# Output stage of a two-branch cross attention: class-token rows of tiles 2 and 3 as a second matmul addend, and a reload split in three

## The reference

```python
query = x @ Wq;  keyt = enc @ Wk;  valt = enc @ Wv        # enc: the first 124 context tokens
hs = mha(query, keyt, valt)                               # 2048 x 640, scores 2048 x 124 a head
ca_q1 = einsum('btc,th->bch', ca, Wq_ca)[:, indices, :]   # 384 rows, spread over 2048
ca_hs1 = mha(ca_q1, x, x)
ca_hs2 = mha(ca_hs1 @ Wq, ca @ Wk_ca, ca @ Wv_ca)         # 4 keys a head
out = (hs + ca_hs2) @ Wout + b_out + x
```

## Time and profile before

| What | Value |
|---|---|
| Runs of the kernel | 767.13, 768.8, 770.88 us (median 768.8) |
| The profiled execution | 769.75 us, span 768.0 us, granted TensorE clock 0.982 |
| Busy: PE, PEld | 725.4 us (94%), 677.1 (88%) |
| Busy: DVE, ACT, POOL | 564.1 us (73%), 375.9 (49%), 171.4 (22%) |
| Output stage of batch 0, of batch 1 | 282 to 417 us, 642 to 768 us |
| DMA | 227021 packets, 82.37 MB; 208324 packets under 512 B |

### The profile page before, as it was taken

How to read it: one execution, slowest core, us unless ns; L and a number is a source line. 1 busy time by engine, 2 the same in 40 slices (tenths; PEclk the granted TensorE clock), 3 DMA queues, 4 the chain that set the end, 5 groups by cost and what they waited for, 6 DMA issues and landing times.

```text
span 768.0 us, 12603 instructions
## 1 busy us (share of the span) xinstructions
PE 725.4 (94%) x4693; PEld 677.1 (88%) x4693; DVE 564.1 (73%) x952; ACT 375.9 (49%) x942; POOL 171.4 (22%) x205
## 2 busy tenths in 40 slices
PE   7998999999899996968999999999999999799998
PEld 5978999999788886968899999999978887699997
DVE  3456888888899997436674888888889998656562
ACT  1634544454588962222333544455479994142330
POOL 8024951222100003502210521111110002211220
PEclk9999999999999999888999999999999999899999
DMA  8424353333400046697754334444230005578852
GB/s 275 144 94 124 69 125 90 90 90 90 145 30 1 0 76 157 137 218 183 151 139 101 65 90 109 102 98 94 90 129 2 0 1 128 131 159 188 177 124 74
DMA packets 227021, 82.37 MB, mean 107 GB/s; under 512 B 208324, under 2 KB 210372, under 8 KB 226960
## 3 DMA queue, kind: packets, MB, share of 16 engines
q1 hardware_dynamic: 226960, 81.56, 43.4%
HBM read 50.06 MB, written 31.39 MB: 106 GB/s over the span
## 4 chain that ended last, share of the span: by engine, by line
PE 80%; DVE 8%; SPq 3%; DMA 3%; issue 3%; ACT 2%; POOL 0%; DVEq 0%; POOLq 0%
PE PS L1230 30%; PE PS L1435 13%; PE PS L1418 6%; PE PS L1205 6%; PE PS L1305 6%; PE PS L1336 6%; PE PS L1327 5%; PE PS L1177 2%; SPq L432 2%; PE PS L1142 2%; DMA exT<-p_kept 2%; DVE pT_lo L1047 1%; SPq L479 1%; DVE res L1063 1%; PE PS L1188 1%
## 5 line engine op out<-in xcount | busy, mean ns | idle before, releaser
L1230 PE MATMUL PS<-mm_hi,xT_hi 128*128 128x280 f32 (+3 forms) x480 | 159.5, 332 | 0.0
L890 DVE TENSOR_REDUCE mpart<-PS 128x4 f32<-128x512 f32 x192 | 131.6, 687 | 36.9 <-PE PS L1205 36.7
L1230 PE MATMUL PS<-mm_hi,xT_lo 128*128 128x280 f32 (+3 forms) x480 | 157.4, 328 | 0.0
L1230 PE MATMUL PS<-mm_lo,xT_hi 128*128 128x280 f32 (+3 forms) x480 | 156.5, 326 | 0.0
L560 POOL TENSOR_TENSOR ex<-ex,rinv 128x992 f32<-128x992 f32 x30 | 55.4, 1845 | 201.5 <-DVE rinv L884 201.4
L666 ACT ACTIVATE ex<-PS,neg 128x124 f32<-128x124 f32 x256 | 89.9, 364 | 11.7 <-DVE gs L872 6.4
L1230 PEld LDWEIGHTS PS<-mm_hi,xT_hi 128*128 128x128 f32 x480 | 90.2, 188 | 0.7 <-issue 0.5
L1230 PEld LDWEIGHTS PS<-mm_lo,xT_hi 128*128 128x128 f32 x480 | 90.4, 188 | 0.3
L1230 PEld LDWEIGHTS PS<-mm_hi,xT_lo 128*128 128x128 f32 x480 | 90.3, 188 | 0.3
L754 ACT ACTIVATE oT_hi<-PS 128x256 fp32r<-128x256 f32 x80 | 29.5, 384 | 121.7 <-PE PS L1418 121.1
L608 POOL TENSOR_TENSOR xin<-xin,bias 128x640 f32<-128x640 f32 x32 | 49.8, 1562 | 160.6 <-DMA xin<-in_x 160.6
(11 more groups left out here) (154 smaller groups left out, 1355.9 us busy)
## 6 DMA issues: line engine op xcount, KB each, us to landing
ex_kept<-ex SPq DMA_DIRECT2D x32, 512.0 KB, 2.9
ex<-ex_kept SPq DMA_DIRECT2D x112, 128.0 KB, 3.1
xin<-in_x SPq DMA_DIRECT2D x128, 80.0 KB, 2.9
xin<-in_x SPq DMA_DIRECT2D x32, 320.0 KB, 3.5
out<-res SPq DMA_DIRECT2D x32, 320.0 KB, 2.3
raw_kept<-raw SPq DMA_DIRECT2D x5, 512.0 KB, 2.6
ex<-ex_kept SPq DMA_DIRECT2D x4, 512.0 KB, 3.8
mm_lo<-raw_kept SPq DMA_DIRECT2D x10, 186.0 KB, 4.4
```

What stands on the lines that cost most here:

```text
L890: nc.vector.tensor_reduce(mpart[:, n // 2, :, 2 * (n % 2):2 * (n % 2) + 2, i].rearrange("p s k -> p k s"), PS[:, 6 + N % 2, :].rearrange(" ...
L1230: last = mul(PS[:, slot(T, k), p0:p0 + w], l[:, i % 2, j, :], rr[:, m0:m0 + w], start=(j == 0 and n == 0), stop=(n == 2), skip_group_check ...
```

## The change

- Tiles 2 and 3 get their image rows as tiles 0 and 1 do. The selection matmul has 512 columns for four tiles; ScalarE copies them to `p2T` and a new `p2T2`; `heads_T(1)` uses 124 rows and adds a matmul of `vcab` and `p2T2` to each of its five parts. Their `gather`, `take_p2c`, `keep_image` and image read are gone: three chunks are left. GpSimd's columns for the next batch wait until `vcab` is read.
- TensorE: nT(1) and nT(2) stand inside output(0, 0), before its fourth part, for after it; the gather of tiles 4 to 7 stands behind output(0, 1) and waits for p2s, for inside group 1.
- VectorE, group 0: after soft2(1) come blocks_T(4), probs2(1), add_x(0), blocks_T(5); add_x(1) stands in group 1 between the second and third oT_lo.
- ScalarE: take_p2c(0) behind soft2(1) in group 0, take_p2c(1) and (2) behind oT_hi of groups 1 and 2.
- SyncE: the block loads of tiles 4 and 5 come before the write back of the last tile, each waiting for a transpose; keep_image(0) and image_rows(2) between the stores of group 0; the block loads of tiles 2g+6 and 2g+7 come behind the stores and the image read of group g.
- The reload of the score matrix: 6, 6 and 3 DMAs behind the block loads of groups 1, 2 and 3, with a semaphore each. next_high and next_low: four in groups 3 to 5 and three in group 6, for three in groups 2 to 6.

The diff, cut to its core:

```diff
--- before.py
+++ after.py
@@ -44,7 +44,8 @@
-CHUNKS = ((2, 4), (4, 8), (8, 12), (12, 16))
+STACKED = 4
+CHUNKS = ((4, 8), (8, 12), (12, 16))
...
@@ -185,6 +186,9 @@
+        with (nc.sbuf_tensor("ns1_room", [P, 2, CAD], F32), nc.sbuf_tensor("p2T_room", [3 * NH * NT, G2], F32R),
+              nc.sbuf_tensor("e0_room", [P, EW], F32), nc.sbuf_tensor("p2T2", [3 * NH * NT, G2], F32R) as p2T2):
+            pass
...
@@ -455,28 +460,32 @@
-                keep_image(0)
+                for i in range(STACKED, STACKED + 2):
+                    sp.wait_ge(exT_made, b * (TILES - OWN) + i - STACKED + 1)
+                    load_blocks(i)
                 sp.wait_ge(norm_made, (b + 1) * TILES)
                 sp.dma_start(ex_kept[b, TILES - 1], last_ex()).then_inc(last_out, 16)
-                image_rows(1)
                 for g in range(GROUPS):
-                    if g + 2 < GROUPS:
-                        if 2 * g + 6 == TILES:
-                            sp.wait_ge(last_out, (b + 1) * 16)
-                        load_blocks(2 * g + 4)
-                        load_blocks(2 * g + 5)
                     store(2 * g)
+                    if g == 0:
+                        keep_image(0)
+                        image_rows(2)
                     store(2 * g + 1)
-                    if g + 1 < GROUPS - 1:
-                        if g < len(CHUNKS) - 1:
-                            keep_image(g + 1)
+                    if 1 <= g < GROUPS - 2:
+                        if g < len(CHUNKS):
+                            keep_image(g)
                         image_rows(g + 2)
-                    if g == 1 and b + 1 < B:
+                    if 2 * g + 6 == TILES - 2:
+                        sp.wait_ge(last_out, (b + 1) * 16)
+                    if g < GROUPS - 3:
+                        for i in range(2 * g + 6, 2 * g + 8):
+                            load_blocks(i)
+                    if 1 <= g < 4 and b + 1 < B:
                         sp.wait_ge(raw_out, KT * 16)
                         sp.wait_ge(nT_ps, CT * (b + 1))
-                        for j in range(KT):
+                        for j in ((0, 1), (2, 3), (4,))[g - 1]:
                             for k, (h0, h1) in enumerate(((6, 8), (0, 3), (3, 6))):
-                                sp.dma_start(mm_heads(mm_lo, j, k).bitcast(F32), raw_kept[:, j * NH + h0:j * NH + h1, 0:NK]).then_inc(raw_in, 16)
+                                sp.dma_start(mm_heads(mm_lo, j, k).bitcast(F32), raw_kept[:, j * NH + h0:j * NH + h1, 0:NK]).then_inc(raw_in[g - 1], 16)
...
@@ -615,6 +624,7 @@
                     if b == 0 and i == 3:
+                        pool.wait_ge(oT_ps, 2 * KT)
                         g_columns(1)
                         y_columns(1)
...
@@ -728,16 +738,20 @@
                     else:
-                        act.wait_ge(image_in, (b * (GROUPS - 1) + i // 2) * 16)
+                        if i < STACKED:
+                            act.wait_ge(exT_made, b * (TILES - OWN) + i - OWN + 1)
+                        else:
+                            act.wait_ge(image_in, (b * (GROUPS - 2) + i // 2 - 1) * 16)
...
 
                 def take_p2T():
-                    act.wait_ge(p2c_ps, b * len(CHUNKS) + 1)
-                    nc.scalar.activation(p2T[:, :], PS[0:3 * NH * NT, 5, 0:G2], ACT.Copy).then_inc(p2T_made, 1)
+                    act.wait_ge(p2T_ps, b + 1)
+                    for to, at in ((p2T, 0), (p2T2, G2)):
+                        nc.scalar.activation(to[:, :], PS[0:3 * NH * NT, 5, at:at + G2], ACT.Copy).then_inc(p2T_made, 1)
 
                 def take_p2c(n):
-                    (i0, i1), (bank, at) = CHUNKS[n], ((5, G2), (4, 0), (5, 0), (4, 0))[n]
+                    (i0, i1), (bank, at) = CHUNKS[n], ((4, 0), (5, 0), (4, 0))[n]
...
@@ -752,8 +766,6 @@
                         nc.scalar.activation(oT_hi[:, j, :], PS[:, oT_bank(g, j), 0:G2], ACT.Copy).then_inc(oTh_made, 1)
-                        if g == 1 and j == 2:
-                            take_p2c(1)
 
...
@@ -766,22 +778,21 @@
                 soft2(0)
                 take_p2T()
-                take_p2c(0)
                 for g in range(GROUPS):
                     oT(g)
                     if g == 1:
+                        take_p2c(1)
+                    if g == 2:
                         take_p2c(2)
-                    if g == 2:
-                        take_p2c(3)
                     if g + 1 < GROUPS:
                         pT(2 * g + 2)
                         pT(2 * g + 3)
                     if g == 0:
                         soft2(1)
+                        take_p2c(0)
                     if b + 1 < B:
-                        if g == 2:
-                            act.wait_ge(raw_in, 3 * KT * 16)
-                        for n in range(3 * g - 6, 3 * g - 3) if 2 <= g < 7 else ():
+                        for n in range(4 * g - 12, min(4 * g - 8, 3 * KT)) if 3 <= g < 7 else ():
+                            act.wait_ge(raw_in[n // 6], (6, 6, 3)[n // 6] * 16)
                             next_high(n)
...
         @block.vector
@@ -1049,6 +1060,8 @@
 
                 def oT(g):
                     for j in range(KT):
+                        if g == 1 and j == 2:
+                            add_x(1)
...
@@ -1091,12 +1104,15 @@
                         soft2(1)
-                    add_x(2 * g_)
-                    if g_ == 0:
+                        dve.wait_ge(pTl_made, b * TILES + STACKED)
+                        blocks_T(4)
                         probs2(1)
-                        add_x(1)
+                        add_x(0)
+                        blocks_T(5)
+                    else:
+                        add_x(2 * g_)
                     if b + 1 < B:
-                        for n in range(3 * g_ - 6, 3 * g_ - 3) if 2 <= g_ < 7 else ():
+                        for n in range(4 * g_ - 12, min(4 * g_ - 8, 3 * KT)) if 3 <= g_ < 7 else ():
                             next_low(n)
...
@@ -1105,7 +1121,7 @@
-                    if g_ + 2 < GROUPS:
+                    if 1 <= g_ < GROUPS - 2:
                         dve.wait_ge(pTl_made, b * TILES + 2 * g_ + 4)
...
@@ -1347,16 +1363,18 @@
-                    (i0, i1), (bank, first) = CHUNKS[n], ((5, G2), (4, 0), (5, 0), (4, 0))[n]
-                    if n >= 2:
-                        pe.wait_ge(p2c_made, b * len(CHUNKS) + n - 1)
+                    (i0, i1), (bank, first) = CHUNKS[n], ((4, 0), (5, 0), (4, 0))[n]
+                    if n == 1:
+                        pe.wait_ge(p2T_made, 2 * (b + 1))
+                    if n == 2:
+                        pe.wait_ge(p2c_made, b * len(CHUNKS) + 1)
...
                             last = mul(PS[0:NH * NT, bank, at:at + w], p2s[:, c, lo, :], sel[:, ms[0]:ms[-1] + 1, :].rearrange("p m n -> p (m n)"),
-                                       skip_group_check=True, start=(n > 0 and c == blocks[0] and lo == 0), stop=(c == blocks[-1] and lo == 1))
+                                       skip_group_check=True, start=(c == blocks[0] and lo == 0), stop=(c == blocks[-1] and lo == 1))
                     last.then_inc(p2c_ps, 1)
...
@@ -1398,11 +1416,10 @@
                     pe.wait_ge(p2l_made, 2 * b + 1)
-                    mul(PS[0:3 * NH * NT, 5, 0:G2], p2s[:, 0].rearrange("p m n -> p (m n)"), sel[:, 0:OWN, :].rearrange("p i n -> p (i n)"),
-                        start=True, stop=True, skip_group_check=True)
-                    gather(0)
+                    mul(PS[0:3 * NH * NT, 5, :], p2s[:, 0].rearrange("p m n -> p (m n)"), sel[:, 0:STACKED, :].rearrange("p i n -> p (i n)"),
+                        start=True, stop=True, skip_group_check=True).then_inc(p2T_ps, 1)
...
-                    pe.wait_ge(p2T_made, b + 1)
+                    pe.wait_ge(p2T_made, 2 * b + 1)
                     for j in range(KT):
...
@@ -1413,14 +1430,15 @@
                         pe.wait_ge(oTl_made, (b * GROUPS + g) * KT + j - 1)
...
                             pe.wait_ge(tmp_made, CT * b + 2 + j)
+                        rows = NK if g == 1 else P
                         for n, (vv, pp) in enumerate(((vs_hi, pT_hi), (vs_lo, pT_hi), (vs_hi, pT_lo))):
                             for k, (h, c0, c1) in enumerate(pieces[j]):
-                                last = mul(PS[:, 6 + j % 2, 0:G2], strip(vv, j, h), pp[:, h, :],
-                                           start=(n == 0 and k == 0), stop=(n == 2 and k + 1 == len(pieces[j])))
+                                last = mul(PS[:, 6 + j % 2, 0:G2], strip(vv, j, h)[0:rows], pp[0:rows, h, :],
+                                           start=(n == 0 and k == 0), stop=(g > 1 and n == 2 and k + 1 == len(pieces[j])))
+                        if g == 1:
+                            pe.wait_ge(p2T_made, 2 * (b + 1))
+                            last = mul(PS[:, 6 + j % 2, 0:G2], vcab[:, j * P:(j + 1) * P], p2T2[:, :], start=False, stop=True)
                         last.then_inc(oT_ps, 1)
```

(20 more changed lines are left out.)

## The result

The changed kernel takes 757.23 us (median of 4, 756.51 to 758.37) against 769.4 of the kernel before beside it (median of 4, 767.13 to 770.88): ratio 0.9846, 95% interval 0.9823 to 0.9869. It is faster, by 1.5%, but by 12 us and not 22, and lies outside my range of 741.5 to 753. The profiled execution took 756.88, with a span of 755.2 and a mean clock of 0.993.

What follows compares the result with a forecast made beforehand. Bound: busy TensorE; only its waits (21.2 us for VectorE's oT_lo) and slow clock give time. 15.0 - 0.3 + 10.2 + 0.4 - 1.2 - 1.7 - 0.1 = 22.3 us gained: 746.5 against median 768.8, range 741.5 to 753.

Steps and rivals of the forecast that it cites:

- group 0 to 1, batch 0: First output matmul of tile pair 0 to that of pair 1: 16.3 us instead of 23.96, gaining 7.7.
- group 2, both batches: Third tile pair: late block loads cost 0.15 us per batch (-0.3); batch 1's old 0.5 wait goes (+0.4).
- group 3: Fourth tile pair, batch 0: block loads ahead of any reload part remove the stall, 14.98 us for 4.75 of work: +10.2.
- group 4: Fifth tile pair, batch 0: late SyncE and VectorE's work make TensorE wait 0.2 to 1.8 us, taken as -1.2.
- group 5: Sixth tile pair, batch 0: TensorE's wait grows to 3.2 us from 1.69, costing 1.7.
- pT_lo starts at 291.9 and ends 2.36 later: VectorE, tiles 2 and 3, batch 0: without the image read, pT_lo ends at 294.2 instead of 298.9.
- TensorE gets to the gather at 290.35 + 8.80 + 0.6: Batch 0: after 60 output matmuls and eight nT, TensorE reaches the gather at 299.8, then waits 0.5 us for p2s.
- land near 314.5, just in time: 0 to 0.5 us of wait in group 2: Block loads of tiles 6 and 7, behind store(1): 0 to 0.5 us wait, taken as 0.15 per batch.
- 4.0 + 15.6: Image read issued 4.0 us after output, then 15.6 to VectorE's oT_lo; less 15.2 cover and 1.2 already waited: 3.2 wait.
- the new wait costs the clock too: Rival, chance 0.25: the 3.2 us wait in group 5 also lowers the clock, losing 2 to 6 us: 749 to 753.
- The prediction's estimate of 750: Two image reads, taken to land after 4 us, could each come up to 1.8 us later, giving 750.
- Not faster: Rival, chance 0.03: each of three reload parts stalls TensorE by 10.2 us, 30.6 against 25.6 gained: 774.

Runs made afterwards that it cites:

- experiment 1: Changed kernel with GpSimd's first three bias additions of each batch held until VectorE's pT_lo of tiles 2 and 3: 760.01 us, ratio 0.9863.
- experiment 2: Kernel before, GpSimd's first bias addition waiting for pT_hi of tile 2, so the additions run beside VectorE's pT_lo: 772.3 us, one run.
- experiment 8: Changed kernel with fixes combined: bias additions after pT_lo, early loads of tiles 6 and 7, reload in five parts of three, first_keys in group 6: 744.28 us.
- experiment 7: Changed kernel with each of its three reload parts ahead of its group's block loads instead of behind: 759.83 us, one run.
- Experiment 5: Changed kernel with bias additions after pT_lo, tile 6's loads ahead of image_rows(2) and tile 7's right behind store(1): 754.45 us, ratio 0.9787.
- experiment 4: Changed kernel without the 15 reload DMAs, GpSimd writing zeros in their place: 752.63 us, one run.
- experiment 9: Changed kernel with only the reload recut, five parts of three DMAs behind groups 0 to 4, three subtractions in groups 2 to 6: 753.22 us, ratio 0.9784.
- experiment 6: Changed kernel with all 15 reload DMAs in one block behind group 1's block loads: 763.29 us, one run.
- experiment 3: Changed kernel with VectorE's first_keys for the next batch moved from group 4 to group 6: 756.67 us, ratio 0.9822.
- 11: Combined kernel (all fixes together) with GpSimd's wait for pT_lo removed again: 746.79 us, ratio 0.9692.

## Why the prediction was wrong

The direction and the places were right; three sizes were not. Against the forecast's sum, from the two timelines (us gained):

| term | forecast | measured |
|---|---|---|
| group 0 to 1, batch 0 | +7.7 | 23.96 - 18.36 = +5.6 |
| group 0 to 1, batch 1 | +7.3 | 23.58 - 18.59 = +5.0 |
| group 2, both batches | -0.3 + 0.4 | -0.5 - 1.0 = -1.5 |
| group 3 | +10.2 | +10.2 |
| group 4 | -1.2 | -1.4 |
| group 5 | -1.7 | 6.3 - 11.4 = -5.1 |
| group 6, and slow start of output(5) | -0.1 | -0.2 |
| sum | 22.3 | 12.6 |

The two spans differ by 12.8.

**Step "pT_lo starts at 291.9 and ends 2.36 later": failed.** The start was right and the duration was not. I took it from a row in which GpSimd was idle and moved the instruction into 4.59 us of add_bias; I had counted GpSimd's new wait and not its old work. Experiments 1 and 2 show it from both sides. The next steps held: from pT_lo's end to the last p2s 6.06 us (295.87 to 301.93) for 6.0, and from gather to output 6.4 for 1.2 + 4.75 + 0.35 = 6.3. In batch 1 most of it stands in the wait: 2.41 for the 0.5 forecast, and 18.6 for 16.3. Alone the two take 2.36 + 4.59 = 6.95 us, together 6.58 from the first start to the last end, so they hardly overlap. The Trainium skill, "SBUF — State Buffer", Who interferes with whom, says that a VectorE instruction with two SBUF inputs contends with a GpSimd instruction that reads SBUF, and calls the port pair that they share an exclusive lock; the trace agrees. The prediction did not reckon with it.

**Same sum, "TensorE gets to the gather at 290.35 + 8.80 + 0.6": failed in batch 0.** It took 11.3 us without the wait, for 9.7 in batch 1, because the clock stood at 0.50 for 3.4 us. That is why p2s was waited for only 0.66 there: a slow TensorE hid a late VectorE. The kernel before has 1.00 in that stretch of both batches. What drops the clock there is open. It fell in no batch of the kernel before and of experiment 2, and in 12 of the 22 batches of the changed kernel and the runs made from it: both in experiments 1 and 8, none in 7, one of the two in every other. In the changed kernel's batch 0 the waits ahead of output(0) hardly differ from before: 0.47, 0.56 and 0.76 us for 0.46, 0.56 and 0.64.

**Step "land near 314.5, just in time: 0 to 0.5 us of wait in group 2": under-sized.** 0.54 and 1.52. The loads stood behind image_rows(2), whose read waits for the write of p_kept: 2.96 us, not 1.6. Experiment 5 removes it.

**Step "4.0 + 15.6" of group 5: its mechanism right, its size wrong.** Issue at +4.4 instead of 4.0, landing 5.68 instead of 4, VectorE's 11.6 as forecast: 21.7, less the 15.2 of cover and the 1.5 already waited in group 4, makes 5.0; it waited 4.83 instead of 3.2. Then the clock, 0.50 over 6.8 us, which is the rival "the new wait costs the clock too" (0.25): true, but with 756.9 beyond its 749 to 753, since the other steps failed too. The prediction's estimate of 750, for reads up to 1.8 later, took its size from the latency at high load in the Trainium skill, "DMA: Bandwidth & Descriptors", Latency and other measured facts; the read of group 5 landed 1.7 later than the 4 that I took, so in size that estimate was nearer for this term. That memory latency is the cause no run shows. Experiments 4 and 9 show that the reload part ahead of the read is: without it, or with three DMAs in it, 4.1 and 4.0.

**Right:** group 3 to a tenth; group 4 (1.50 us of wait for 1.2, of which experiment 4 puts 1.2 down to the reload part); "Not faster" refuted; no loss in the later groups of batch 1. **Wrong in the weighing:** each step had a cover of under 1 us, and I gave the errors as independent of one another in a range 11.5 us wide, where late DMA moves groups 2, 4 and 5 together.

## What to carry to other kernels

An instruction that is moved brings its duration only if the other engines' work at the new place is the same: look up what GpSimd does there before a VectorE operation with two SBUF inputs is moved, and the other way round. The same holds for the fix: GpSimd's additions, held back behind pT_lo, met the next such VectorE operation, a small one (0.23 us became up to 1.50), where the chain could not spare it. A transfer taken off the head of a queue should be cut so fine that a part ends before the next short, urgent read is due; here 15 reload DMAs in parts of three cost the combined kernel no wait in groups 3 to 5, in parts of six about 5 us there (1.2 and 3.8, experiment 4), and as one block 9 to 10, ahead of the loads (14.98 for 4.75) or behind them (336.7 to 359.6 from output to output in experiment 6, for 13.5). A wait that a fix removes may reappear as a low clock or as the next wait, so judge a fix together with the others: GpSimd's wait alone brought nothing (760.0 for 757.2), in the combined kernel 2.5 us by the medians, with overlapping intervals.

## What the runs showed of the hardware

- VectorE's pT_lo (two of 128x1024, both inputs in SBUF) takes 2.36 us alone, 4.21 to 4.77 beside add_bias that began first, 3.73 where the two began within 0.2 us; add_bias (three of 128x640) 4.59 alone and 6.4 to 6.6. A subtraction of 128x64 with both inputs in SBUF takes 0.23 alone and, where add_bias runs already, ends with it: 0.57 to 1.50. Two multiplications of 128x192 with one input in PSUM take 0.80 to 0.85 either way.
- In the chains of these runs an image read lands after 3.3 to 4.6 us with no reload or a part of three ahead, and after 4.75 to 6.27 with six just ahead of it and the stores.
- How long a wait must be to cost the clock had no sharp edge. It stayed whole behind waits of 1.50, 2.05 (experiment 3), 2.26, 2.38, 2.41, 2.57 and 2.87 us, and fell behind 1.80 (experiment 9), 2.14 (11), 2.75 (1), 2.94, 3.28, 3.52, 4.06 and 4.83. 2.05 us also cost it in experiment 7, whose window from 2 us behind that wait shows 0.56, the 1.2 GHz level; the second line is the window behind the 1.80 of experiment 9:

```profile
355.90:359.30 3.40, 3.40 (x17) 3.40 (x17) 0.85 (x2) 1.40 (x3) 0.76 (x1) 0.56 1.00 236
...
665.50:668.90 3.40, 3.40 (x20) 3.40 (x21) 0.95 (x3) 0.77 (x2) 1.41 (x1) 0.66 0.77 229
```
